# Second residual by a ScalarE copy and an accumulating DMA, one buffer for the transformed rows, and a new order of work, in a two-layer convolution kernel

## What is computed

```python
def gn(v):              # 32 groups of 4 channels: (v - mean) / sqrt(var + 1e-5)
    ...
def layer0(x):          # x already normalised
    v = round(clip(x * input_factor, -1, 1) * 127) / 127 * 0.6
    v = pad(swapaxes(v, -2, -1), 1)
    fv = v + 0.1 * v ** 3
    outs = [conv3x3(fv, g_pos[i] - g_neg[i]) for i in range(3)]      # 128 -> 128 channels
    mem = adc(outs[2]) + 4 * adc(outs[0]) + 2 * adc(outs[1]) + adc(outs[2])
    return transpose(mem * output_factor + bias)
def layer1(x):          # x: [b, 128, 4096], Wq, Wk, Wv: 64 x 128
    q, k, v = Wq @ x, Wk @ x, Wv @ x
    num, den = exp(B) @ (exp(k) * v), exp(B) @ exp(k)
    return Wm @ (q * num / den)
x = x + layer0(gn(x))
x = x + layer1(gn(x))   # the residual that the change is about
```

## Time and profile before

| what | us |
|---|---|
| median of 3 runs (lowest, highest) | 1651.25 (1646.66, 1653.33) |
| the profiled execution, and its span | 1651.83, 1649.9 |
| TensorE busy | 1503.9 (91%) |
| VectorE busy | 1469.2 (89%) |
| ScalarE busy | 1061.9 (64%) |
| GpSimd busy | 676.7 (41%) |
| second residual on VectorE, 122 passes | 77.8 |
| TensorE waits for the second residual, 28 times | 48.1 |

### The profile page before, as it was taken

How to read it: one execution, slowest core, us unless ns; L and a number is a source line. 1 busy time by engine, 2 the same in 40 slices (tenths; PEclk the granted TensorE clock), 3 DMA queues, 4 the chain that set the end, 5 groups by cost and what they waited for, 6 DMA issues and landing times.

```text
span 1649.9 us, 21257 instructions
## 1 busy us (share of the span) xinstructions
PE 1503.9 (91%) x7024; PEld 648.5 (39%) x7024; DVE 1469.2 (89%) x2093; ACT 1061.9 (64%) x1391; POOL 676.7 (41%) x565
## 2 busy tenths in 40 slices
PE   1499999999999999999999999999999999999875
PEld 1244434344343444444344444434443443434332
DVE  4759999998989999898999999899998989999665
ACT  4447766675767766676776667577666757665344
POOL 2311444363444436353443634344363535435212
PEclk9799999999999999999999999999999999999997
DMA  5010100201020020102002010200201020000001
GB/s 192 1 51 16 37 13 27 77 27 64 27 77 26 14 77 28 65 26 77 26 14 77 27 64 28 78 26 14 77 26 65 26 77 26 13 26 26 26 39 51
DMA packets 20537, 72.34 MB, mean 44 GB/s; under 512 B 3072, under 2 KB 3264, under 8 KB 20416
## 3 DMA queue, kind: packets, MB, share of 16 engines
q1 hardware_dynamic: 20416, 70.86, 11.8%
HBM read 37.29 MB, written 33.55 MB: 43 GB/s over the span
## 4 chain that ended last, share of the span: by engine, by line
PE 54%; DVE 34%; issue 9%; ACT 2%; POOL 1%; DVEq 0%; DMA 0%; SPq 0%; POOLq 0%; ACTq 0%
PE A L455 8%; PE A L456 8%; PE A L457 8%; PE L L509 7%; PE B L455 6%; PE B L456 5%; PE B L457 5%; DVE duo L931 3%; DVE t L943 3%; DVE duo L978 3%; DVE duo L979 2%; DVE uall L1009 2%; PE L L551 2%; DVE f L908 2%; DVE xr L1043 2%
## 5 line engine op out<-in xcount | busy, mean ns | idle before, releaser
L455 PE MATMUL A<-T,WH 128*128 128x504 f16 (+1 forms) x1152 | 438.4, 381 | 0.9 <-ACT uall L699 0.9
L457 PE MATMUL A<-T,WL 128*128 128x504 f16 (+1 forms) x1152 | 437.4, 380 | 0.0
L456 PE MATMUL A<-T,WH 128*128 128x504 f16 (+1 forms) x1152 | 437.3, 380 | 0.0
L1240 POOL TENSOR_TENSOR T<-t,T 128x512 f16<-128x512 f32 x192 | 235.6, 1256 | 395.7 <-ACT T L657 395.7
L1232 POOL TENSOR_TENSOR zl<-zf,zh 128x512 f16<-128x512 f32 x120 | 185.8, 1548 | 376.6 <-ACT zh L719 369.5
L675 ACT ACTIVATE junk<-xr,shift 128x1024 f16<-128x1024 f32 x256 | 293.8, 1148 | 13.7 <-DVE xr L1012 6.2
L455 PE MATMUL B<-T,WH 128*128 128x504 f16 (+1 forms) x576 | 223.0, 387 | 32.7 <-POOL T L1240 20.5
L456 PE MATMUL B<-T,WH 128*128 128x504 f16 (+1 forms) x576 | 222.2, 386 | 0.0
L457 PE MATMUL B<-T,WL 128*128 128x504 f16 (+1 forms) x576 | 221.7, 385 | 0.0
L1227 POOL TENSOR_SCALAR zf<-xr,rs,bi 128x512 f32<-128x512 f32 x124 | 189.7, 1530 | 18.0 <-POOL zl L1232 13.7
L455 PEld LDWEIGHTS A<-T,WH 128*128 128x128 f16 x1152 | 114.2, 99 | 188.0 <-issue 74.3
(11 more groups left out here) (152 smaller groups left out, 2375.5 us busy)
## 6 DMA issues: line engine op xcount, KB each, us to landing
xr<-in_x_dram SPq DMA_DIRECT2D x64, 512.0 KB, 6.0
out_dram<-xr SPq DMA_DIRECT2D x64, 512.0 KB, 2.7
xr<-in_L_conv_g_pos_dram SPq DMA_DIRECT2D x3, 576.0 KB, 9.9
xr<-in_L_conv_g_neg_dram SPq DMA_DIRECT2D x3, 576.0 KB, 10.6
xr<-in_L_conv_Wm_dram SPq DMA_DIRECT2D x2, 32.0 KB, 9.7
xr<-in_L_conv_Wq_dram SPq DMA_DIRECT2D x1, 32.0 KB, 11.3
xr<-in_L_conv_Wk_dram SPq DMA_DIRECT2D x1, 32.0 KB, 11.1
xr<-in_L_conv_Wv_dram SPq DMA_DIRECT2D x1, 32.0 KB, 10.8
```

The costliest lines, as they stand in the source:

```text
L455: nc.tensor.matmul(to, wh, th, start=fresh and y == 1, stop=False, skip_group_check=True)
L456: nc.tensor.matmul(to, wh, tl, start=False, stop=False, skip_group_check=True)
L457: done = nc.tensor.matmul(to, wl, th, start=False, stop=y == 2, skip_group_check=True)
L1240: last = nc.gpsimd.tensor_tensor(low, t32[:, pair, :, :, :].rearrange("p t e w -> p (t e w)"), high, ALU.subtract)
```

## The change

The second residual leaves VectorE. ScalarE copies the mix, scaled by 1/64, from both banks of L into one of two SBUF buffers y2 (evict, position 8), and GpSimd issues a DMA that adds y2 onto the quarter of xr (add_mix, position 8 too). TensorE's next keys_values now waits for the copy (evicted), SyncE's store for the addition (y_added). Only the last image keeps second_residual.

The transformed rows T are one buffer for all images, not one for even and one for odd; ScalarE's rows_high therefore also waits until the image before has been convolved so far. The freed space (`shared`) holds y2, and ek, ekv, rec and zf. GpSimd's work now follows slots as the other engines' does, with add_mix in it, and scale_x ahead of z_low(3). Many slots are moved; FIRST goes from 20 to 22. Phases 2 to 5 are unrolled too.

```diff
-FIRST = 20
+FIRST = 22
...
-L2_ACT = (1, 3, 5)
-L2_DVE = (1, 4, 6, 8)
-X_STATS = (1, 2, 4, 6)
+L2_ACT = (1, 3, 5, 8)
+L2_DVE = (2, 5, 6)
+L2_POOL = (6, 8)
+X_STATS = (1, 3, 4, 6)
...
-COMBINE = (18, 0)
+COMBINE = (20, 2)
...
-TRANSFORM = (26, 32, 2, 9)
-HIGH = (27, 33, 3, 11)
+TRANSFORM = (27, 32, 2, 12)
+HIGH = (29, 32, 6, 14)
...
-        T = [sb(f"T{i}", [P, 2, 3, H // 4, 2, W], F16) for i in range(2)]
+        T = sb("T", [P, 2, 3, H // 4, 2, W], F16)
+
+        shared = sb("shared", [P, NP * 4 * 3 * P + 4 * 3 * P])
+        y2 = [shared[:, k * PX:(k + 1) * PX] for k in range(2)]
+        second = [shared[:, 4 * PX + k * HALF:4 * PX + (k + 1) * HALF] for k in range(4)]
...
-            with eng.Fori(2, B - 5, RING) as p:
+            for p in range(2, 2 + RING):
+                phase(p, p % RING, (True, True, True, True))
+            with eng.Fori(2 + RING, B - 5, RING) as p:
...
-                sp.wait_ge(second_done, nth(image, NG, k))
+                if isinstance(image, int) and image == B - 1:
+                    sp.wait_ge(second_done, k + 1)
+                else:
+                    sp.wait_ge(y_added[k % 2], nth(image, 32, 16 * (k // 2) + 15))
...
-                    pe.wait_ge(second_done, nth(image, NG, k - 1))
+                    pe.wait_ge(evicted, nth(image, NG, k - 1))
...
+                if not (isinstance(image, int) and image == 0):
+
+                    act.wait_ge(conv_ready, nth(image, STEPS, NP * (g // 2 + 1) - 1, 1))
...
+            def evict(image, k):
+
+
+                act.wait_ge(mix_ready, nth(image, NG, k))
+                if k >= 2 or not (isinstance(image, int) and image == 0):
+                    act.wait_ge(y_added[k % 2], nth(image, 32, 16 * (k // 2) - 1))
+                nc.scalar.activation(y2[k % 2], last_pair[:, :, :].rearrange("p a n -> p (a n)"), ACT.Identity,
+                                     scale=1.0 / WSCALE).then_inc(evicted, 1)
...
-                if at == L2_DVE[3]:
-                    second_residual(image, m, k, 0)
...
+            def add_mix(image, m, k):
+
+                waits_apart(pool, (evicted, nth(image, NG, k)))
+                nc.gpsimd.dma_start(xr[m][:, k * PX:(k + 1) * PX], y2[k % 2], accum_op=ALU.add
+                                    ).then_inc(y_added[k % 2], 16)
+
+            def second_layer(image, m, c):
+
+                k, at = divmod(c, CYCLE)
+                if at == L2_POOL[0] and k < NG - 1:
+                    z_low(image, m, k + 1, 0)
+                if at == L2_POOL[1]:
+                    add_mix(image, m, k)
...
-                if prev and cur:
-                    z_low(p - 1, before, 0, 0)
-                    z_low(p - 1, before, 1, 0)
...
+                for slot in range(SLOTS):
+                    late, soon = second_places(p, slot)
+                    if prev2:
+                        for c in late:
+                            second_layer(p - 2, two_before, c)
+                    if prev and cur and slot == FIRST - 1:
+                        z_low(p - 1, before, 0, 0)
+                    if prev and cur:
+                        for c in soon:
+                            second_layer(p - 1, before, c)
```

More of the change, by code:

```diff
@@ L55 @@
 X_MOMENTS = 9
-COMBINE = (18, 0)
-DOUBLE = (14, 32)
+COMBINE = (20, 2)
+DOUBLE = (12, 33)
 RESIDUAL = (25, 7)
-BIAS = (16, 30)
-X1_STATS = (26, 29, 9, 10)
+BIAS = (18, 32)
+X1_STATS = (26, 30, 9, 13)
 X1_SPREAD = 14
 X1_GROUP = 15
+LOW = (28, 33, 7, 11)
 X1_MOMENTS = 15
@@ L128, in conv_layers_kernel @@
         junk = sb("junk", [P, PX], F16)
-        zf = sb("zf", [P, HALF])
-        last_t = T[0][:, :, :, :, :, :].rearrange("p a b c d e -> p (a b c d e)")
+        zf = second[3]
+        last_t = T[:, :, :, :, :, :].rearrange("p a b c d e -> p (a b c d e)")
         last_f = f[:, :, :].rearrange("p r w -> p (r w)").bitcast(F16)
         def work(name, dt, size):
-            first = sb(name, [P, size], dt)
+            first = sb(name, [P, size], dt) if dt == F16 else second[("ek", "ekv", "rec").index(name)]
             half_words = size * (2 if dt == F32 else 1)
-            out = [first[:, :]]
+            out = [first[:, :] if dt == F16 else first]
             src, at = (last_f, free_f) if name == "rec" else (last_t, free_t)
@@ L452, in taps @@
                     wh, wl = WH[:, plane, y, j, :], WL[:, plane, y, j, :]
-                    th, tl = (T[parity][:, part, pair, tiles, e, y - 1 + lo:y - 1 + hi] for part in range(2))
+                    th, tl = (T[:, part, pair, tiles, e, y - 1 + lo:y - 1 + hi] for part in range(2))
                     to = out[:, :, lo:hi]
@@ L550, in mix @@
                     half = slice(h * IC, (h + 1) * IC)
-                    last = nc.tensor.matmul(banks[w][1 - h], wmf[half, :], rec[w][half, :], start=True, stop=True)
+                    last = nc.tensor.matmul(banks[w][h], wmf[half, :], rec[w][half, :], start=True, stop=True)
                 last.then_inc(mix_ready, 1)
@@ L1042, in second_residual @@
                     xh = xr[m][:, (2 * k + h) * HALF:(2 * k + h + 1) * HALF]
-                    last = nc.vector.scalar_tensor_tensor(out=xh, in0=banks[w][1 - h], scalar=1.0 / WSCALE,
+                    last = nc.vector.scalar_tensor_tensor(out=xh, in0=banks[w][h], scalar=1.0 / WSCALE,
                                                           in1=xh, op0=ALU.mult, op1=ALU.add)
@@ L1237, in rows_low @@
                     waits_apart(pool, (th_ready, nth(image, NP * NG, NP * g + pair)))
-                    high, low = (T[parity][:, part, pair, g * TILES:(g + 1) * TILES, :, :]
+                    high, low = (T[:, part, pair, g * TILES:(g + 1) * TILES, :, :]
                                  .rearrange("p t e w -> p (t e w)") for part in range(2))
@@ L1246, in phase @@
                 before, two_before = (m + 3) % RING, (m + 2) % RING
[L1247 to L1267 removed]
+                for slot in range(SLOTS):
[8 more added lines that the diff above has]
+                            second_layer(p - 1, before, c)
+                    if cur and slot in LOW[2:]:
+                        rows_low(p, m % 2, LOW.index(slot))
+                    if nxt and slot in LOW[:2]:
+                        rows_low(p + 1, 1 - m % 2, LOW.index(slot))
+                    if nxt and slot == X_MOMENTS:
+                        scale_x(p + 1)
+                    if prev and slot == X1_MOMENTS:
+                        scale_z(p - 1)
                 if not cur:
```

37 lines of the change are left out of this document (11 added, 26 removed).

## The result

The changed kernel takes **1690.72 us** (median of 4 runs, 1689.75 to 1692.28), the kernel before 1651.85 us beside it: a ratio of **1.0238**, 95% interval 1.0225 to 1.0252. It is slower, by more than the forecast 1672 us and inside the range. The profiled execution has a span of 1688.0 us, 38.1 us over the one before.

The account below looks back on a forecast made before the run. TensorE, busy 1151.97 of 1200 us in the steady part, was taken as the bound. From 1651.83 us, -50.7 + 49 + 18 + 4 = +20 gave 1672 us, range 1628 to 1708.

Parts of the forecast that it names:

- Its main step: Quarter 0: TensorE's low-part matmuls wait for GpSimd's z_low, queued behind the waiting DMA; 3.5 us once an image, +49 us.
- What it removes: TensorE's 28 waits of keys_values for the second residual, 48.1 us, go with two half-clock stretches of 1.3 us: -50.7 us.
- The 2.9 us of cover: Copies of quarters 1 and 2 cost nothing; only a ScalarE later than 2.9 us would cost the difference.
- The chain: Last mix to quarter 0's low part: copy start 1.5, copy 1.0, handover 0.1, issue 1.0, z_low 5.8, less 5.94: 3.5 us.
- The rival in which VectorE stretches the issue: GpSimd's DMA issue is held up by a VectorE integer pass of 0.68 us: wait 4.2 us, 1682 us, chance 0.10.
- The half clock: TensorE falls to 1.2 GHz behind the new wait in each of 14 images, 1.3 us each: +18 us.
- The weighting behind transform(1): Quarter 1's weighted values on VectorE stand behind transform(1), which waits for GpSimd's rows_low(0): 0.3 us an image, +4 us.
- The rival that priced this chain at 1.5 us an image: transform(1) and the weighting cost 1.5 us an image, not 0.3: +17, 1689 us, chance 0.08.
- "Nothing in sum" for what is moved: Other passed queues hold up nothing; later loop entry against a slightly longer end comes to nothing in sum.
- VectorE's relief "counts nothing more": VectorE's 77 us of saved residual passes count nothing more, since no other listed TensorE wait hangs on VectorE.

## Why the prediction came out as it did

Its main step was right in place, mechanism and nearly in size: one wait of the low parts an image, behind evict, the DMA and four passes. The forecast was 19 us too low by sizes beside it.

- **What it removes** held: no wait for the residual, and no wait of TensorE for a copy of another quarter. The 2.9 us of cover was enough.
- **The chain** was put at 9.4 us and took 9.67, the wait at 3.5 and took 3.57. Several terms were off and cancelled. The copy starts 1.17 us behind the mix and not 1.5, since cubic(0) is over (782.10) when the mix ends: combine_planes took 2.46 us on VectorE (778.05 to 780.51) where 3.30 had been read from one image of before. The handover to the DMA is 0.56 us, five times the 0.1 that the sum had. The issue holds the next pass up for 0.66 us and not 1.0. z_low needs 6.2 and not 5.8, with one pass at 2.05 us. TensorE needs the low part 6.10 us after the mix's start and not 5.94. The rival in which VectorE stretches the issue did not come, and was not put to the test: the issue takes 0.95 us here beside its mean of 917 ns, but in none of its 60 places in this trace does a tensor_scalar pass of VectorE lie beside it.

```profile
L1272 POOL DMA_DIRECT2D xr<-shared x60 | 55.0, 917 | 147.4 <-ACT shared L755 147.4
```

- **The half clock** was taken as paid by every image, which twelve of thirteen did, but its size of 1.3 us came from one pair of images behind a 2.2 us wait. Here it is 1.6 us: 3 us more over the run. The clock did fall nearly always behind 3.5 to 3.6 us and never behind 1.18; even so one wait of 3.58 us left it alone.
- **The weighting behind transform(1)** failed in its mechanism and, with it, in its size: 0.3 us forecast, 1.03 measured, 12.2 us instead of 4. The rival that priced this chain at 1.5 us an image gave 1689, near the measured time, but by the same wrong cause. It was not GpSimd's signal that came late; mix_middle, which the sum did not list since the weighting stood behind it before as well, took 7.85 us (808.47 to 816.32) instead of 4.7, because GpSimd's rows_low(0) now falls beside it. Before, the three passes took 0.68 or 0.69 us each (896.88 to 898.77), and rows_low was over at 896.16. The prediction knew the stretch for GpSimd's passes and did not turn it round.
- **"Nothing in sum" for what is moved** missed small new waits: group statistics 35.5 us over the span, against 32.3 before, and quarter 2's queries 3.7 us against 1.0.
- **Sum by these rows:** -50.7, +51.2 of the chain, +21 of half clock (13 times 1.6), +12.2, +3.2, +2.7, and -3.9 at the mix (L563, 2.8 us where L551 waited 6.7): +35.7 of the 38.1 us. That is closer than it should be: with the smaller rows the two lists come to 138.8 us before and 151.9 us after, which together with the clock makes +31.5, so that 6.6 us stand in no row.
- **VectorE's relief "counts nothing more"** is wrong for the new order, as the run with the residual back on VectorE shows: 24 us slower although the chain is gone, in part by the transform that it brings beside z_low(1). Whether it holds for the order of before no run shows.

What the prediction did not ask is what the step would be worth with the chain gone. It treated the new order as given and the wait as its price; moving two calls by two slots makes it a gain of 29 us.

## What to carry to other kernels

A DMA issued from a compute engine's queue carries that queue's wait: look at what stands behind it there, and put work that needs nothing of it ahead. When a copy takes a step's place on a critical bank, ask of each engine that feeds the next user of the bank whether its own preparation still runs ahead of the copy. And when work on GpSimd or VectorE moves, look at which VectorE passes with two SBUF inputs and which GpSimd passes now run beside each other: this had a part in the changed kernel and in the losses of three of the experiments, and the order of a queue alone does not show it.

## What the runs showed of the hardware

- An accumulating SBUF to SBUF DMA of 512 KB, issued from GpSimd, took 0.92 us in GpSimd's row, let the next pass start 0.66 us after its own start, began 0.56 us after the end of the ScalarE pass that it waited for, and landed 4.6 us after the issue (the page's DMA rows, median of 60):

```profile
xr<-shared POOLq DMA_DIRECT2D x60, 512.0 KB, 4.6
```

- GpSimd's three passes over 128x512 beside VectorE's two-input SBUF passes took 4.74 us, and those of VectorE 1.65 instead of 0.69 us. Even at 128x8 the three GpSimd passes took 1.86 us in their row, 0.6 us each, so that a small pass there is not free.
- VectorE's two small statistics passes of 128x1 and 128x4 took 0.22 and 0.23 us with GpSimd idle, and 1.07 and 0.96 us beside GpSimd's rows_low.
- Behind nearly the same wait (3.5 to 3.6 us) TensorE's half-clock stretch cost nothing in one image, 1.5 to 1.7 us in eleven and 2.5 us in one, and up to 2.9 us in the kernel with short rows_low; behind 1.18 us there was none in thirteen images. 24 matmuls an image that do nothing new in the wait won 17 us.
